# Attention-value products on four 32-column tiles, with the values of four batches placed in SBUF by eight transfers

## What is computed

```
def _L0_xattn_ref(x, y, wq, bq, wk, bk, wv, bv, wo, bo):     # N_HEADS = 16, DIM_HEAD = 16
    q = (x @ wq + bq).reshape(B, Sq, H, D).transpose(0, 2, 1, 3)
    k = (y @ wk + bk).reshape(B, -1, H, D).transpose(0, 2, 1, 3)
    v = (y @ wv + bv).reshape(B, -1, H, D).transpose(0, 2, 1, 3)
    scores = jnp.einsum('bhqd,bhkd->bhqk', q, k) / jnp.sqrt(jnp.asarray(D, x.dtype))
    attn = jax.nn.softmax(scores, axis=-1)
    out = jnp.einsum('bhqk,bhkd->bhqd', attn, v)
    return out.transpose(0, 2, 1, 3).reshape(B, Sq, E) @ wo + bo
x = x + jnp.tanh(g_xattn[0]) * _L0_xattn_ref(_layernorm(x, axis=-1), ctx_768, ...)
x = x + jnp.tanh(g_ffn[0]) * _L0_ffn_ref(_layernorm(x, axis=-1), ...)
```

## Time and profile before

| | |
|---|---|
| median of 3 runs | 341.96 us (340.11 to 343.99) |
| span of the profiled execution, first to last instruction | 339.1 us |
| instructions in it | 7286 |
| mean granted TensorE clock | 0.980 of full |
| HBM read, written | 21.20 MB, 9.85 MB |
| DMA packets | 38150, of which 16608 under 512 B |
| share of the chain that ended last | PE 61%, DVE 15%, ACT 8%, issue 7%, DMA 5% |

### The profile page before, as it was taken

One profiled execution on the slowest core, in us unless ns is written; L12 is line 12 of the kernel. 1 busy time (PEld: TensorE's weight loads), 2 busy tenths in 40 slices (PEclk: granted clock), 3 DMA queues, 4 the chain that ended last, 5 costly groups with the idle time before them and its releaser, 6 DMA issues.

```text
span 339.1 us, 7286 instructions
## 1 busy us (share of the span) xinstructions
PE 318.2 (94%) x2363; PEld 282.2 (83%) x2363; DVE 227.9 (67%) x516; ACT 215.6 (64%) x483; POOL 184.0 (54%) x261
## 2 busy tenths in 40 slices
PE   6997879899999999999999999999999999999993
PEld 5764666678988877788799889999999999999992
DVE  6999689999878899796767675534333544353463
ACT  2855898976786665658957584547546546464652
POOL 8226979885652564757371177432255536534542
PEclk9998599999999999999999999999999999999997
DMA  7992855274422030053160100315246233212300
GB/s 191 299 340 38 241 126 160 42 198 128 109 80 56 2 97 29 0 139 121 15 240 2 62 2 31 127 32 188 79 168 217 66 151 93 77 35 75 92 32 28
DMA packets 38150, 35.68 MB, mean 105 GB/s; under 512 B 16608, under 2 KB 35060, under 8 KB 37613
## 3 DMA queue, kind: packets, MB, share of 16 engines
q1 hardware_dynamic: 34568, 27.36, 28.5%
q0 software_dynamic: 2720, 7.32, 6.4%
q10 hardware_dynamic: 837, 0.67, 0.8%
HBM read 21.20 MB, written 9.85 MB: 92 GB/s over the span
## 4 chain that ended last, share of the span: by engine, by line
PE 61%; DVE 15%; ACT 8%; issue 7%; DMA 5%; POOL 1%; POOLq 1%; SPq 1%; DVEq 0%; ACTq 0%
PE y_ps L1535 20%; PE h_ps L1535 17%; PE bank L1535 9%; PE s_ps L1535 9%; DMA x_all<-in_x 5%; PE bank L1668 4%; ACT probs L947 2%; DVE rsum L1264 2%; DVE smax L1246 1%; DVE probs L1258 1%; DVE stats L1147 1%; DVE other_sum L1232 1%; ACT pT L956 1%; DVE hT_lo L1469 1%; ACT xn L898 1%
## 5 line engine op out<-in xcount | busy, mean ns | idle before, releaser
L690 POOL TENSOR_TENSOR probs<-probs,rinv 128x616 f32<-128x616 f32 x32 | 39.1, 1223 | 37.8 <-DVE rinv L1268 37.5
L1535 PE MATMUL y_ps<-sw,hT_hi 128*128 128x256 f32 x272 | 57.1, 290 | 1.2 <-DVE hT_lo L1513 1.2
L1535 PE MATMUL y_ps<-ew,hT_hi 128*128 128x256 f32 x256 | 54.1, 286 | 1.8 <-DVE hT_lo L1469 1.7
L1469 DVE TENSOR_TENSOR hT_lo<-h,hT_hi 128x256 fp32r<-128x256 f32 x64 | 29.2, 457 | 38.5 <-ACT h L1086 35.2
L1535 PEld LDWEIGHTS y_ps<-sw,hT_hi 128*128 128x128 f32 x272 | 44.9, 191 | 2.9 <-DVE hT_lo L1513 1.8
L1535 PEld LDWEIGHTS y_ps<-ew,hT_hi 128*128 128x128 f32 x256 | 42.4, 188 | 3.0 <-DVE hT_lo L1469 3.0
L1535 PE MATMUL h_ps<-x2T_hi,sw 128*128 128x512 f32 (+1 forms) x160 | 43.6, 359 | 0.1
L1083 ACT ACTIVATE hT_hi<-h_ps,vec_cols 128x256 fp32r<-128x256 f32 x32 | 15.2, 475 | 39.5 <-PE h_ps L1535 35.3
L995 ACT ACTIVATE hT_hi<-h_ps,vec_cols 128x512 fp32r<-128x512 f32 (+1 forms) x40 | 24.6, 614 | 21.9 <-PE h_ps L1535 17.3
L1535 PE MATMUL y_ps<-sw,hT_lo 128*128 128x256 f32 x136 | 38.4, 282 | 0.0
L1535 PE MATMUL y_ps<-ew,hT_lo 128*128 128x256 f32 x128 | 35.9, 280 | 0.0
(11 more groups left out here) (206 smaller groups left out, 837.1 us busy)
## 6 DMA issues: line engine op xcount, KB each, us to landing
v_diag<-v_rows SPq DMA_DIRECT2D x16, 256.0 KB
stage<-in_L_ffn_w SPq DMA_DIRECT2D x4, 1024.0 KB, 5.6
sw<-ew SPq DMA_DIRECT2D x4, 1024.0 KB
xs<-sorted_dram SPq DMA_DIRECT2D x8, 257.0 KB
stage<-in_L_ffn_sw SPq DMA_DIRECT2D x2, 1024.0 KB, 6.6
x_all<-in_x SPq DMA_DIRECT2D x1, 1536.0 KB, 9.8
part_dram<-x_all SPq DMA_DIRECT2D x3, 512.0 KB, 2.9
k_dram<-probs SPq DMA_DIRECT2D x2, 616.0 KB, 5.9
```

Source lines behind the costliest of these rows:

```text
L690: nc.gpsimd.tensor_tensor(pq, pq, rinv[:, b % 2, k, :].unsqueeze(2).to_broadcast([P, HG, KEYS]), ALU.mult).then_inc(p_ready, 1)
L1469: nc.vector.tensor_tensor(hT[1][:, c % HB, 0:RTOK], h32[:, c % 2, 0:RTOK], hT[0][:, c % HB, 0:RTOK], ALU.subtract).then_inc(h_lo, 1)
L1535: return nc.tensor.matmul(out_, lhsT, rhs, start=start, stop=stop, **kw)
```

## The change

- The columns of the probabilities are stored in another order: within each half of a group the two pairs of heads alternate (a step of two elements, 8 bytes, from one key to the next), by the view `heads_of`. It is used where the scores are shifted or exponentiated into `probs`, summed and divided. The exponential at L937 works on the whole row as before.
- `turn` reads chunks 0 to 3 with that step of two (128 columns: the first 128 of a pair's 154), and chunk 4, the 4 x 26 keys that are left, as 104 neighbouring columns.
- `attend` has for each group four products of 32 output columns, one for each pair of heads, on four column tiles, and one of 128 columns for what is left.
- The values of all eight batches have room of their own, `v_pair` and `v_left`. There is no DRAM tensor for them, and `vz` and `vw` are gone. `vr.0` and `vr.1` each place four batches from SBUF to SBUF with eight transfers: four to `v_pair` with 77, 51, 51 and 77 rows of 16 runs of 64 bytes, and four to `v_left` with 26 rows of 8 runs of 64 bytes.
- `v32` is now two buffers, one of them in `h32`. So `he.0` waits for the second share's transfers, the rows of b2 moved to `other_sum`, and `yT` moved to `pT`.
- POOL clears both `v_pair` and `v_left` in six memsets after its constants, before `bl`.
- SP's list: `kw.1` comes right behind `kw.0`; `wd.0` and `wd.1` stand before `vr.0`; `vr.1` is behind `kr.3`.

The core of the diff:

```diff
-MIDDLE = CHUNKS // 2
-ROWS = [GK - (CHUNKS - 1) * P if c == MIDDLE else P for c in range(CHUNKS)]
-ROW0 = [sum(ROWS[:c]) for c in range(CHUNKS)]
+PAIRS = HG // 2
+HP = PAIRS // 2
+PK = 2 * KEYS
+LEFT = PK - P
+ROWS = [P] * PAIRS + [PAIRS * LEFT]
+PD = 2 * HEAD_DIM
...
-    fl.0 kw.0 vz.0 vz.1 kw.1 kr.1 kr.2 wd.0 vw.0 wd.1 vw.1 vr.0 kr.3 vw.2 vr.1 vr.2 kr.4 vw.3 wd.3 vw.4 vr.3
-    kr.5 vr.4 wd.2 vw.5 vw.6 vr.5 kr.6 vw.7 ps.0 kr.7 vr.6 vr.7 ps.1 wd.4 wd.5 ps.2 ps.3 xs ps.4
+    fl.0 kw.0 kw.1 kr.1 kr.2 wd.0 wd.1 vr.0 kr.3 vr.1 kr.4 wd.3 kr.5 wd.2 kr.6 ps.0 kr.7 ps.1 wd.4 wd.5 ps.2 ps.3 xs ps.4
...
-        v_diag = sb("v_diag", [P, 2, CHUNKS, GROUPS, P], scope=att)
+        v_pair = sb("v_pair", [P, 2, BATCHES, GROUPS * HP, PD], scope=att)
+        v_left = sb("v_left", [P, BATCHES, GROUPS, P], scope=att)
...
-        yT = v_diag[0:CK + 1, 1, :, :, :].rearrange("p c g f -> p (c g f)")[:, 0:CKC * BATCHES * KEYS].rearrange(
+        v32 = [held[0:KEYS, :, :].rearrange("k a c -> k (a c)").rearrange("k (m b d) -> k m b d", m=2, b=VALUE_BATCHES)
+               for held in (v_first, h32)]
+        yT = pT[0:CK + 1, :, :].rearrange("p c s -> p (c s)")[:, 0:CKC * BATCHES * KEYS].rearrange(
...
+        def heads_of(b, k):
+
+            return probs[:, b % 2, k, :].rearrange("p (n q k i) -> p n i q k", n=2, q=2, i=HP)
+
+        def by_head(rows):
+            return rows.rearrange("p (n i q) -> p n i q", n=2, q=2)
...
-            def zero_values(n):
-
-                sp.wait_ge(cleared[1], 1)
-                sp.wait_ge(x_in[2], 16)
-                sp.dma_start(v_dram[n, 0:(CHUNKS - 1) * P].rearrange("(c p) g f -> p c (g f)", p=P),
...
-            def values_out(b):
-
-                n = b % 2
-                sp.wait_ge(v_32, b // 2 + 1)
...
-                for g in range(GROUPS):
-                    diagonal = bass.AP(v_rows, n * GK * GROUPS * P + g * P,
-                                       [[GROUPS * P, KEYS], [KEYS * GROUPS * P + HEAD_DIM, HG], [1, HEAD_DIM]])
-                    sp.dma_start(diagonal, v32[:, b // 2, n, g * P:(g + 1) * P].rearrange("k (h f) -> k h f", h=HG)
-                                 ).then_inc(v_out[n], 16)
...
+            def values_in(share):
+
+                batches = slice(share * VALUE_BATCHES, (share + 1) * VALUE_BATCHES)
+                sp.wait_ge(cleared[1], 3 * (share + 1))
+                sp.wait_ge(v_32, (share + 1) * VALUE_BATCHES // 2)
+                split = P - KEYS
+                for half, parity, to, key in ((0, 0, 0, 0), (0, 1, KEYS, 0), (1, 0, 0, LEFT), (1, 1, split, 0)):
+                    rows = KEYS if half == parity else split
+                    heads = v32[share][key:key + rows, half, :, :].rearrange("k b (c q f) -> k (b c) q f", q=2, f=HEAD_DIM)
+                    cols = slice(parity * HEAD_DIM, (parity + 1) * HEAD_DIM)
+                    sp.dma_start(v_pair[to:to + rows, half, batches, :, cols].rearrange("p b c f -> p (b c) f"),
+                                 heads[:, :, parity, :]).then_inc(v_in[share], 16)
+                for half in range(2):
+                    key = split if half == 0 else 0
+                    left = v32[share][key:key + LEFT, half, :, :].rearrange("k b (g d) -> k (b g) d", g=GROUPS)
+                    for i in range(HP):
+                        first = (2 * i + 1 - half) * HEAD_DIM
+                        rows = slice(half * HP * LEFT + i, (half + 1) * HP * LEFT, HP)
+                        sp.dma_start(v_left[rows, batches, :, half * HR + first:half * HR + first + HEAD_DIM].rearrange(
+                                     "p b g f -> p (b g) f"), left[:, :, first:first + HEAD_DIM]).then_inc(v_in[share], 16)
...
-            nc.gpsimd.memset(v_diag[:, 0, :, :, :], 0.0).then_inc(cleared[1], 1)
+
+            def clear_values(share):
+
+                batches = slice(share * VALUE_BATCHES, (share + 1) * VALUE_BATCHES)
+                for half in range(2):
+                    nc.gpsimd.memset(v_pair[:, half, batches, :, :], 0.0).then_inc(cleared[1], 1)
+                nc.gpsimd.memset(v_left[:, batches, :, :], 0.0).then_inc(cleared[1], 1)
...
+            for share in range(2):
+                clear_values(share)
...
-                pq = probs[:, b % 2, k, :].rearrange("p (h k) -> p h k", k=KEYS)
-                nc.gpsimd.tensor_tensor(pq, pq, rinv[:, b % 2, k, :].unsqueeze(2).to_broadcast([P, HG, KEYS]),
-                                        ALU.mult).then_inc(p_ready, 1)
+                pq = heads_of(b, k)
+                inverse = by_head(rinv[:, b % 2, k, :]).unsqueeze(4).to_broadcast([P, 2, HP, 2, KEYS])
+                nc.gpsimd.tensor_tensor(pq, pq, inverse, ALU.mult).then_inc(p_ready, 1)
...
-                    ins = nc.scalar.activation(to[:, h * KEYS:(h + 1) * KEYS], score_banks(quarter)[:, h // HH, keys],
+                    ins = nc.scalar.activation(heads_of(b, k)[:, h // HH, h % HH // 2, h % 2, :],
+                                               score_banks(quarter)[:, h // HH, keys],
                                                ACT.Exp, bias=smax[:, b % 2, k, h:h + 1])
...
                 if q == 0:
                     act.wait_ge(rows_ready, 2)
+                    act.wait_ge(v_in[1], 16 * VALUE_LOADS)
...
-                nc.vector.tensor_reduce(out=rsum[:, b % 2, k, :],
-                                        in_=probs[:, b % 2, k, :].rearrange("p (h k) -> p h k", k=KEYS),
-                                        axis=AX_X, op=ALU.add).then_inc(p_sum, 1)
+                nc.vector.tensor_reduce(out=by_head(rsum[:, b % 2, k, :]), in_=heads_of(b, k), axis=AX_X, op=ALU.add
+                                        ).then_inc(p_sum, 1)
                 dve.wait_ge(p_sum, 4 * b + k + 1)
...
+                        if c < PAIRS:
+                            first = c // HP * (GK // 2 + HP * LEFT) + c % HP
+                            cols = slice(first, first + HP * (P - 1) + 1, HP)
+                        else:
+                            cols = slice(HP * P, HP * P + ROWS[c])
                         ins = nc.tensor.transpose(bank[m][0:ROWS[c], v * SEQ + t * P:v * SEQ + (t + 1) * P],
-                                                  probs[:, b % 2, g * TB + t, ROW0[c]:ROW0[c] + ROWS[c]], ident[:, :])
+                                                  probs[:, b % 2, g * TB + t, cols], ident[:, :])
...
-                pe.wait_ge(v_in[b % 2], 16 * 3 * (b // 2 + 1))
+                pe.wait_ge(v_in[b // VALUE_BATCHES], 16 * VALUE_LOADS)
                 pe.wait_ge(pT_sb, TURNS * (b + 1))
                 for g in range(GROUPS):
-                    for n in range(MIDDLE):
-                        for half in range(2):
-                            c, cols = half * (MIDDLE + 1) + n, slice(half * HR, (half + 1) * HR)
-                            mm(bank[m][cols, g * SEQ:(g + 1) * SEQ], v_diag[:, b % 2, c, g, cols],
-                               pT[:, g * CHUNKS + c, :], g == 0 and n == 0, False, skip_group_check=True)
+                    for i in range(PAIRS):
+                        cols = slice(i * PD, (i + 1) * PD)
+                        mm(bank[m][cols, g * SEQ:(g + 1) * SEQ], v_pair[:, i // HP, b, g * HP + i % HP, :],
+                           pT[:, g * CHUNKS + i, :], g == 0, False, skip_group_check=True)
                 for g in range(GROUPS):
-                    ins = mm(bank[m][:, g * SEQ:(g + 1) * SEQ], v_diag[0:ROWS[MIDDLE], b % 2, MIDDLE, g, :],
-                             pT[0:ROWS[MIDDLE], g * CHUNKS + MIDDLE, :], False, True, skip_group_check=True)
+                    ins = mm(bank[m][:, g * SEQ:(g + 1) * SEQ], v_left[0:ROWS[PAIRS], b, g, :],
+                             pT[0:ROWS[PAIRS], g * CHUNKS + PAIRS, :], False, True, skip_group_check=True)
```

55 lines of the change are left out of this document (15 added, 40 removed).

## The result

| | kernel before | changed kernel |
|---|---|---|
| median | 341.55 us (20 runs) | 345.28 us (20 runs) |
| ratio | 1 | 1.0103, 95% interval 1.0079 to 1.0127 |
| span of the profiled execution | 339.1 us | 341.7 us |
| mean granted TensorE clock in it | 0.980 | 0.985 |

Every ratio in this document compares the fast runs of a kernel with fast runs of the kernel before made beside them, so it can differ a little from the quotient of two medians. The change costs 3.5 us. The forecast was 338.2 us, its range ended at 344.5. The two profiled executions are 2.6 us apart; the changed kernel's took 343.44 us, 1.8 less than its median. The first fence is the page's busy times of the changed kernel, against the earlier trace rows; in it PE has 2 us less work and 2.6 us more time.

A forecast was written before the change was run, and what follows sets the result against it. PE was taken to bound the kernel in part, ACT and DVE elsewhere: 341.96 - 3.5 (products on the chain) - 0.9 (the others) + 0.6 (wait for first values) = 338.2 us; range 334.5 to 344.5, the forecast's own 336.5 to 340.0.

The forecast's parts named there:

- POOL's clearing, cost 0: POOL's start: memsets of 4.2 us delay its loads, but its 4.75 us wait for ACT hides that; cost 0.
- The value products: PE's eight value products, 42 to 192 us: each falls from 3.01 to 2.14 us; 4.4 us off in sum.
- rival (d): PE's value products: the four tiles run only two at a time; 342.6 us, or 342.0 without the wait; chance 0.08.
- PE's work counts in full for four batches of eight: Four value products are pieces of the chain that ended last, so their whole saving counts: 3.5 us.
- Rival (a): Value products: all eight count, 7.0 us off and no wait for the first values; 335.0 us, chance 0.16.
- The other order of the columns: The 8-byte step in DVE's sum, POOL's division, the writes and PE's weight load in the turning: cost taken as 0.
- The upper end (13 us): PE's turnings: the step doubles the weight load, 0.14 to about 0.28 us, costing up to 13 us of PE.
- rival (c): The 8-byte step costs: 344.8 us at its upper end on PE, near 341 on other engines; chance 0.10.
- SP's list: cost 0: SP's issues: 44 gone, 16 added; transfers queued behind vr.0 have several us of cover, so cost 0.
- The landing of the first values: First value product, near 50 us: its values land at 51.8 us, 51.2 would cost nothing; a wait of 0.6 us.
- X: Time in us for the packets of vr.0, the first share's transfers, before the first value product; taken as 9.8 us.
- Rival (b): First value product: the values land late and hold PE's list; 344.4 us at 16 us of packets; chance 0.16.

The follow-up runs named there:

- before_short: The kernel before without eight of the sixteen 64-column matmuls in each value product (for the time alone): 337.16 us, ratio 0.9935.
- before_clears: The kernel before with eight more POOL memsets of 128x512 at the place where the changed kernel has its six: 345.97 us, ratio 1.0187.
- before_gains_early: The kernel before with its one memset moved behind the iotas, so POOL's loads of the gains are issued earlier: 343.90 us, ratio 1.0106.
- split_order: The changed kernel with three memsets before the gains' loads, three behind the last keys_lo step, and DVE's ot.0.1 behind x1.4.1: 342.02 us, ratio 1.0049.
- clear_late: The changed kernel with POOL's six memsets moved behind the last keys_lo step: 346.33 us, ratio 1.0193.

## Why the prediction was wrong

**POOL's clearing, cost 0: this step failed, twice.** The count of work was right (memsets 3.74 us, forecast 4.2), and so was the cover: POOL's first keys_lo came only 1.9 us later, behind ACT. But I asked only who waits for POOL. First, DVE doesn't wait for POOL by any semaphore and was held all the same, until the last memset ended. The Trainium skill ("SBUF — State Buffer", "Terms", the shared port pair) says that DVE and GpSimd share ports by an exclusive lock, held for the full instruction, on which the loser fully blocks. The row agrees that DVE is blocked (1.84 us for 0.21) and goes beyond one instruction: three memsets ended before DVE did. It was there to be weighed in the forecast. Second, I took away a memset of 1.17 us and wrote it off as a saving. It was what kept two tiny loads from being issued 1.1 us earlier: taking that delay alone out of the kernel before costs 1.0106, in its profile with a stretch at half clock. In the changed kernel the two lie side by side, together 2.9 us: at 12 us the hold alone makes PE 1.50 us late and both 1.85.

**The value products: right in the instruction, wrong in the term.** 2.13 us against 2.14 forecast: four tiles of 32 columns do run at once, and rival (d) is out. The step that failed is "PE's work counts in full for four batches of eight", plus a quarter for the rest: 4.4 us. before_short measures 2.2. A product that is a piece of the chain gives up its time only until the next engine becomes the chain. DVE had 18.7 of 20 and 26.65 of 30 us of work in two stretches, and PE's waits for ACT and DVE, 1.0 and 0.6 us in the kernel before, about doubled. Nor did the four products counted in full come through: from 50 to 216 us before_short gains only 1.6 us, less than half of their 3.5. In the changed kernel's chain of waits only one value product is left as a whole piece, the last:

```profile
189.14 2.06 PE bank L1534 x20
```

Rival (a), all products, is the farther off for it.

**The other order of the columns: half right.** DVE's sum (786 ns), POOL's division (1234) show no cost, so the Trainium skill's rule on cachelines ("SBUF — State Buffer"), by which the 8-byte step keeps its rate, agrees with them. For PE's weight load it doesn't: 192 ns for 142. It stays under the 0.2 us that I had named as the sign of a wrong step, and cost 0.7 to 1.75 us all the same, by the traces. The upper end (13 us) and rival (c) at 344.8 assumed a doubling; it was a third more.

**SP's list: cost 0 held,** though the eight transfers took SP 14.4 us to issue where a load of keys takes 0.7. kr.3 went out at 49.63 us in place of 44.45, and no wait of PE for it shows.

**The landing of the first values: right in size, 0 instead of 0.6 us.** X was 9.8 us (packets from 41.3 to 51.0 us), as forecast, and that is in part luck: the forecast spread them over 5.5 engines, while the last 3 us went at the pace of SP's issues. The product waited 0.67 us for ACT as before, since the whole start was 2 us late and covered it. With the start mended, the wait came up at once in one version (1.95 us). The Trainium skill's rule on engines ("DMA: Bandwidth & Descriptors", "Why a DMA increments its semaphore by 16 and not by 1") agrees in direction: with 48 rows in one transfer, the 1209 packets of 43 to 46 us became 1485. But the tail is SP's issuing. Rival (b) didn't happen.

**The sum.** With the measured terms: 341.96 - 2.2 (products) + 2.9 (start) + 0.7 to 1.75 (stride) + 0 (landing) = 343.4 to 344.4. Measured is 341.96 x 1.0103 = 345.5. The 1.1 to 2.1 us left are within the intervals of the terms (the first alone is 0.9 to 3.5, the second 1.5 to 4.3). The traces, taken alone, close up to 216 us: 2.06 late at 50 us, 1.6 less for short products, 1.6 to 1.75 more for the stride give 2.0 to 2.2, and the changed kernel is 2.21 late. Its last matmul is 2.54 late, so no trace here shows what is left, and its cause is open. Behind 216 us two things vary. Up to 230 us about 1 us comes back in each version with the changed placing and in before_short (-2.20 to -1.23), where PE waits 0.7 to 0.9 us for ACT; but in before_clears too. And the gather near 235 us was late in six of the eleven kernels with the changed placing and in none of the six with the old one; it was not late in the changed kernel's own profile. Neither was tried by itself.

Two numbers of the forecast were off without changing it. The 2.9 us "around the span" compare a median with one execution; where time and span are of the same execution they are 1.7 us apart (343.44 and 341.7). And the forecast's own range, 336.5 to 340.0, isn't what the bounds named for it give, which is 335.0 to 339.1.

## What to carry over

Before a wait is called cover, ask what else the covered engine shares: memsets on POOL in its idle time held a DVE instruction for 1.84 us in the changed kernel, and for 2.97 us in before_clears, which took 1.9% longer. An instruction that is taken away from in front of a DMA is a transfer moved earlier; look at what other traffic it now meets. And price a shortened piece of the chain by the slack of the next engine in that stretch, not by its own length: here 2.2 of 7.0 us came through. And before a clock of 1.00 is believed at the very start of a trace, compare the spacing of equal matmuls.

## What the runs showed of the hardware

- A DVE TENSOR_SCALAR of 128x2, SBUF to SBUF, that meets a row of POOL memsets isn't let in between two of them: it ended within 0.05 us of the last one's end, 1.84 us (changed kernel) or 2.97 us (before_clears) long. BATCH_NORM_STATS2 at 5.51 us, under the same memsets, took its usual 0.75 for two.
- With two loads of 512 bytes to 128 partitions issued by POOL at 1.95 us instead of 3.05, all queues together moved 95 GB/s instead of 256 over 6 to 8 us (before_gains_early), with the DMA engines 0.37 busy. The mechanism is open.
- A weight load of 128 fp32 columns with a step of 8 bytes takes 190 to 193 ns where neighbouring columns take 138 to 142, in every kernel of this study.
- The plain fp32 matmuls of 32 columns ran four at a time on four column tiles: sixteen of them and four of 128 columns took 2.13 us, where sixteen of 64 columns on two tiles and the same four took 3.01.
- PE began each traced execution at half pace: equal matmuls start twice as far apart at first (identity matmuls 0.21 us, later 0.11), with the change at 4.5 us in the kernel before, 14.0 in split_order and 18.1 in clear_late, where the trace's first record of its clock stands.
